# A GRU over 256 steps with an eight-expert layer beside it: first expert products in column groups, one a step

## The chip, the cores and the metric

The kernel runs on one core of a Trainium2 chip. The metric is the device time of one execution in microseconds (us). Three executions of the kernel before took 1025.38, 1026.15 and 1026.09 us, a median of 1026.09 us.

Engines are named as the profile names them: PE is TensorE's matmul side and PEld its weight loads, DVE is VectorE, ACT is ScalarE, POOL is GpSimd, SP is SyncE.

## What is computed

`x` has the shape 16 x 256 x 512 (batch, time, features). A GRU cell runs over the 256 time steps, and its states go through a mixture of eight low-rank experts, of which each token uses the two with the largest router values. The result is added to `x`:

```python
def cell(h, x):
    gi = x @ W_ih + b_ih
    gh = h @ W_hh + b_hh
    r = sigmoid(i_r + h_r)
    z = sigmoid(i_z + h_z)
    n = tanh(i_n + r * h_n)
    return (1.0 - z) * n + z * h
...
router_logits = h / norm(h) @ router_w            # 8 experts, softmax, top 2, renormalised
for e in range(8):
    out = out + combine[:, e, None] * (h @ Wa[e] @ Wb[e])    # 512 -> 128 -> 512
x = x + out
```

Every step needs the state of the step before, so the 256 steps are a chain. The experts do not feed back into it.

## The kernel before, in words

**Numbers in two parts.** Operands of the products are kept as pairs of fp16 numbers, a high and a low part, and each product is three products (`TERMS`: high-high, high-low, low-high). Where two successive products of a pair use the same stationary operand, the second one is a matmul without a weight load (`matmul_held`, line 840); the others go through line 849.

**Steps and blocks.** Eight time steps (S = 8) times 16 batch rows make a block of 128 tokens; there are NB = 32 blocks. In the text "step s" is a time step n with n % 8 = s. PE's program for a step n is: `state_part(n)`, then `wide_step(n)` if n is odd, `grouped_step(n)` if n is even (lines 1081 to 1087).

`state_part(n)` multiplies the state by W_hh. The 16 batch rows of the two parts give 32 stationary columns, so four matmuls, each on 32 columns of the array and 32 partitions of PSUM, run beside each other; I call such four a **quad**. There are 4 quads of 256 moving columns with the first state operand (line 929, which needs `st` from DVE line 762 and the bank seeded by ACT line 570), 4 with the second (line 934), and 8 of 128 columns for the z gate (`zbank`), of which every second is held.

`pair_ahead(n)` computes the input side of the gates for two steps at once, three steps ahead. One pair of steps is 12 **units**, a unit being a quad of 384 columns. `FIRST_UNITS = (3, 5, 5)` says how many units stand in the odd step that begins a pair; the even step after it does the rest. So step 3 has 3 units and step 4 has 9, and all other odd steps have 5 and even steps 7.

The experts' **first products** (`expert_down`, 512 -> 128, one call for one expert and one block) are 12 matmuls of 128 x 128 weights on the whole array, with 128 moving columns, into `ybank`. `DOWN` places them two at a time in steps 1, 3, 5 and 7. The **second products** (`expert_up_by_tokens`, 128 -> 512) are 3 terms of a quad of 512 columns, into `nbank` or `obank`. `UP` places them two at a time in steps 4, 6, 0 and 2. In an odd step the order on PE is state part, router (step 3 alone, `route`), first products, units; in an even step it is state part, units, second products. The last two steps and `last_experts` finish the last block.

**The other engines.** DVE's `gru_step` (lines 732 to 764) transposes the gates' bank (`tr`, line 734), adds the two halves of the r gate (line 737), transposes and adds the rest (740, 742, 745), multiplies by r (749, `rhn`), adds the input's part (753, `npre`), and after ACT's tanh makes the new state (758 `u`, 762 `st`, 763, 719). ACT's `gru_step` makes r (598, `rr`), z (604), 1 - z (606, `omz`), tanh (608, `nn`), and seeds the banks of the next step (570, 577). Each engine then does the `beside(n)` work:
- DVE: turn the input side of the n gate (769), `add_expert(n - 12)` (798, `acc`, one expert a step, on the result of the second product), and in step 3 the two largest router values (776, 778).
- ACT: in even steps the biases (589); in step 7 the squares (617); for every first product `split_y`, two activations (643 and 647); in step 0 two gathers of 512 columns (623); in step 3 `weigh` (638), which waits for POOL's `gaps`; step 2 and 6 convert x.
- POOL: for every first product `low_y` (459), the low part of y; in steps 4 and 6 half of the low part of x (434); in steps 0 to 4 the norm and the router's small work.

Two waits of DVE are touched by the change. Before `npre` (line 753) stand two waits, for `n_turned` (line 751) and for `rhn_ready` (line 752); before `u` (line 758) stands one, for `n_ready`:

```python
dve.wait_ge(n_turned, n // 2 + 1)
dve.wait_ge(rhn_ready, n + 1)
nc.vector.tensor_tensor(npre[:, :, :], rhn[:, :, :], gi_n[...], ALU.add)
...
dve.wait_ge(n_ready, n + 1)
nc.vector.scalar_tensor_tensor(out=u[:, :], in0=nn[:, :], ...)
```

Of the kernel before, what the change touches and what calls it, by code (L numbers as in the profile page):

```python
# [12 lines left out]
P = 128  # L13
# [15 lines left out]
def gru_moe_kernel(nc, x, cond, W_ih, W_hh, b_ih, b_hh, router_w, Wa, Wb, out):  # L29
# [4 lines left out]
    NB = T // S  # L34


    DOWN = (9, 9, 11, 11, 13, 13, 15, 15)
    UP = (12, 12, 14, 14, 16, 16, 18, 18)
    FIRST_UNITS = (3, 5, 5)
    ADD = S + 4  # L40
    YB = 6

    AHEAD = 3
# [9 lines left out]
    with ExitStack() as ctx:  # L53
# [106 lines left out]

        def downs_at(n):

            return [n - DOWN[e] + e for e in range(NE) if DOWN[e] % S == n % S and n >= DOWN[e]]

        def ups_at(n):
# [235 lines left out]
        def _(pool):  # L401
# [100 lines left out]
            def beside(n):  # L502
                i, s = n // S, n % S
                if s == 0 and 1 <= i:
                    fold_squares(i - 1)
                    add_squares(i - 1)
                if s in (1, 2) and 1 <= i:
                    less_upper_half(i - 1, s - 1)
                if s == 3 and 1 <= i:
                    invert_norm(i - 1)  # L510
                if s == 4 and 1 <= i:
                    combine(i - 1)
                if s in (4, 6) and 1 <= i and i + 2 < NB:
                    split_x(i + 2, s // 6, n)
                for m in downs_at(n):
                    low_y(m)
                if s == 3 and 1 <= i:
                    gaps(i - 1)
# [19 lines left out]
        def _(act):  # L538
# [57 lines left out]
            def gru_step(n):  # L596
# [2 lines left out]
                                     scale=1 / PROD_SCALE).then_inc(r_ready, 1)  # L599
                if n % S == 3 and n >= S:  # L600
                    read_router(n // S - 1)
                act.wait_ge(z_summed, n + 1)
                zpre = pre[:, ZG, :, :].rearrange("p k b -> p (k b)")
                nc.scalar.activation(zz[:, :, :].rearrange("p k b -> p (k b)"), zpre, ACT.Sigmoid,  # L604
# [44 lines left out]
            def beside(n):  # L649
                i, s = n // S, n % S  # L650
                if s % 2 == 0 and n + 4 < T:
                    put_biases(n // 2 + 2)
                if s == 7:
                    square(i)
                for m in downs_at(n):
                    split_y(m)
                if s == 0 and 1 <= i:
                    for part in range(2):
                        gather_states(i - 1, part)
                if s == 3 and 1 <= i:  # L660
                    weigh(i - 1)
                if s == SPLIT_AT and i + 3 < NB:
                    split_x(i + 3)
                if s == SCALE_AT and 1 <= i and i + 2 < NB:
                    scale_x(i + 2)
                if n == 0:
                    split_first(2)
                if 0 <= n < len(SPLITS) - N_GRU_SPLITS:
                    split_weights(N_GRU_SPLITS + n)
# [34 lines left out]
        def _(dve):  # L704
# [27 lines left out]
            def gru_step(n):  # L732
# [15 lines left out]
                dve.wait_ge(r_ready, n + 1)  # L748
                nc.vector.tensor_tensor(rhn[:, :, :].rearrange("p k b -> p (k b)"), rr[:, :],
                                        pre[:, HN, :, :].rearrange("p k b -> p (k b)"), ALU.mult).then_inc(rhn_ready, 1)  # L750
                dve.wait_ge(n_turned, n // 2 + 1)
                dve.wait_ge(rhn_ready, n + 1)
                nc.vector.tensor_tensor(npre[:, :, :], rhn[:, :, :], gi_n[:, n // 2 % 2, :, n % 2 * B:(n % 2 + 1) * B],
                                        ALU.add).then_inc(npre_ready, 1)
                dve.wait_ge(z_ready, n + 1)
                nc.vector.tensor_tensor(v[:, :, :], zz[:, :, :], hist[:, past(n - 1), :, (n - 1) % S, :], ALU.mult)
                dve.wait_ge(n_ready, n + 1)
                nc.vector.scalar_tensor_tensor(out=u[:, :], in0=nn[:, :], scalar=PART_SCALE, in1=omz[:, :],  # L758
                                               op0=ALU.mult, op1=ALU.mult).then_inc(u_ready, 1)
# [77 lines left out]
        def _(pe):  # L837
# [108 lines left out]
            def route(f):  # L946
# [5 lines left out]
                if f == NB - 1:  # L952
                    pe.wait_ge(acc_done, LEFT - 1)
                else:
                    pe.wait_ge(yhi_ready, f * NE + 2)
                    pe.wait_ge(y32_ready, f * NE + 2)

                wait(pe, router_read, f)
                pe.wait_ge(sq_step, (f + 1) * SQ_STEPS)
# [12 lines left out]
            def wait_first_product(m):  # L972
                f, e = m // NE, m % NE

                wait(pe, yhi_ready, m - 1)
                wait(pe, y32_ready, m - 1)
                if e == 3 and f < NB - 1:
                    pe.wait_ge(router_read, f + 1)
                if e == 0:
                    pe.wait_ge(both_parts_ready, 2 * ((f + 1) * S + 1))  # L980
                if m in wa_split_at:
                    pe.wait_ge(weights_split, splits_before(wa_split_at[m]))

            def expert_down(m):
# [3 lines left out]
                for k in range(K):  # L988
                    for pw, ph in TERMS:
                        mm = product((pw, ph) == (0, 1), y_at(m)[:, 0:P], wa[:, pw, k, e, :],  # L990
                                     hparts[:, f % HB, k, :, ph * B:(ph + 1) * B], n == 0, n == 3 * K - 1)
                        n += 1
                mm.then_inc(y_done, 1)

# [35 lines left out]

            def pair_ahead(n):

                if n + AHEAD < T:
                    first = FIRST_UNITS[0 if n % S in (3, 4) else 2 if n % S in (7, 0) else 1]
                    pair_part((n + AHEAD) // 2, range(first) if n % 2 else range(first if n else 6, K * len(TERMS)))

            def wide_step(n):
                i, s = n // S, n % S
# [2 lines left out]
                for m in downs_at(n):  # L1041
                    expert_down(m)
                pair_ahead(n)

            def grouped_step(n):
                pair_ahead(n)
                for m in ups_at(n):
                    expert_up_by_tokens(m)
                if n == 0:
# [31 lines left out]
            grouped_step(0)  # L1081
            for n in range(1, T):
                state_part(n)
                if n % 2:
                    wide_step(n)
                else:
                    grouped_step(n)
# [23 lines left out]
```

## Time and profile before

| | |
|---|---|
| median of three runs | 1026.09 us |
| the profiled execution, its own time | 1025.33 us |
| its span, first to last instruction | 1023.5 us |
| mean granted TensorE clock | 0.996 of 2.4 GHz |
| busy: PE, PEld | 987.4 us (96%), 669.4 us (65%) |
| busy: DVE, ACT, POOL | 879.4 us, 692.9 us, 287.9 us |

The time of the profiled execution is the span and 1.8 us around it. A busy PE counts each matmul's whole stay in the pipeline (a quad of 128 columns shows 0.22 us while a new quad starts every 0.056 us), so 96% does not say that PE has no room: the starts of its instructions have to be read. The granted clock is full speed but for the start and the last microseconds.

### The profile page before, as it was taken

What the parts mean: (1) busy time and instruction counts of PE and PEld (TensorE: products, weight loads), DVE (VectorE), ACT (ScalarE), POOL (GpSimd) and SP (SyncE); (2) the same over time, 40 slices, a digit from 0 to 9 for tenths busy, and PEclk for the clock granted to TensorE, in tenths of its full rate; (3) what the DMA queues carried; (4) which work ended last, traced back from release to release, by engine and by line L of the source; (5) the groups of instructions that cost most, each with busy time, mean ns of one, the idle gap of its engine ahead of it and who ended that gap; (6) DMA issues with size and microseconds to landing.
All of it is one profiled execution on the core that took longest, in us unless ns stands there. A gap on an engine that the chain in (4) does not pass through costs nothing.

```text
span 1023.5 us, 60856 instructions
## 1 busy us (share of the span) xinstructions
PE 987.4 (96%) x29067; PEld 669.4 (65%) x20799; DVE 879.4 (86%) x3631; ACT 692.9 (68%) x2696; POOL 287.9 (28%) x729
## 2 busy tenths in 40 slices
PE   4789999999999999999999999999999999999997
PEld 2455666666667666666666666666666666666664
DVE  6889888888888888888888888888888888888886
ACT  6677666676766676666677666667666767766663
POOL 1032233232323322323332332332233322223223
PEclk9999999999999999999999999999999999999999
DMA  8321111111111111111101111101111101110000
GB/s 297 88 80 29 30 32 29 26 31 31 28 32 32 27 27 34 27 30 33 28 25 35 29 31 29 32 25 33 29 29 33 30 24 32 30 30 19 14 9 28
DMA packets 49361, 38.84 MB, mean 38 GB/s; under 512 B 34532, under 2 KB 38972, under 8 KB 49084
## 3 DMA queue, kind: packets, MB, share of 16 engines
q1 hardware_dynamic: 48236, 31.41, 11.3%
q8 instruction: 198, 3.24, 1.3%
q10 hardware_dynamic: 848, 3.54, 1.0%
q14 instruction: 79, 0.65, 0.2%
HBM read 18.94 MB, written 8.39 MB: 27 GB/s over the span
## 4 chain that ended last, share of the span: by engine, by line
PE 89%; DVE 6%; DMA 2%; issue 1%; ACT 1%; SPq 0%; POOL 0%; DVEq 0%; POOLq 0%; ACTq 0%
PE pairs L849 16%; PE ybank L849 12%; PE gates L929 12%; PE gates L934 11%; PE pairs L840 7%; PE ybank L840 6%; PE zbank L849 5%; PE zbank L840 5%; PE obank L849 5%; PE nbank L849 5%; PE obank L840 2%; PE nbank L840 2%; DMA whh<-in_L_cond_W_hh 1%; DVE acc L798 1%; DVE tr L734 1%
## 5 line engine op out<-in xcount | busy, mean ns | idle before, releaser
L849 PE MATMUL pairs<-wx,xs 128*32 128x384 f16 x4096 | 281.9, 328 | 0.2 <-DVE wx L714 0.2
L598 ACT ACTIVATE rr<-pre 128x64 f32<-128x64 f32 x256 | 65.2, 255 | 203.0 <-DVE pre L737 202.9
L849 PE MATMUL ybank<-hparts,wa 128*128 128x128 f16 x2048 | 193.9, 219 | 0.6 <-ACT y L647 0.6
L459 POOL TENSOR_TENSOR y<-y 128x128 f16<-128x128 f32 x256 | 105.6, 433 | 276.2 <-ACT y L647 274.8
L849 PEld LDWEIGHTS ybank<-hparts,wa 128*128 128x128 f16 x2048 | 159.9, 98 | 30.1 <-issue 16.0
L840 PE MATMUL ybank<-hparts,wa 128*128 128x128 f16 x1024 | 178.2, 219 | 0.0
L840 PE MATMUL pairs<-wx,xs 128*32 128x384 f16 x2048 | 175.1, 327 | 0.0
L929 PE MATMUL gates<-whh,st 128*32 128x256 f16 x4080 | 157.8, 273 | 17.3 <-DVE st L762 15.9
L849 PEld LDWEIGHTS pairs<-wx,xs 128*32 128x32 f16 x4096 | 109.6, 97 | 94.2 <-issue 54.7
L929 PEld LDWEIGHTS gates<-whh,st 128*32 128x32 f16 x4080 | 98.3, 96 | 97.2 <-ACT gates L570 86.2
L934 PE MATMUL gates<-whh,hparts 128*32 128x256 f16 x4080 | 158.2, 273 | 0.0
L849 PE MATMUL zbank<-whh,hparts 128*32 128x128 f16 x4080 | 146.4, 219 | 0.0
L840 PE MATMUL zbank<-whh,hparts 128*32 128x128 f16 x4080 | 146.4, 219 | 0.0
L734 DVE STREAM_TRANSPOSE tr<-gates 128x256 f32<-128x256 f32 x256 | 114.5, 447 | 20.5 <-PE gates L934 17.5
L849 PEld LDWEIGHTS zbank<-whh,hparts 128*32 128x32 f16 x4080 | 116.1, 97 | 12.9
L934 PEld LDWEIGHTS gates<-whh,hparts 128*32 128x32 f16 x4080 | 112.9, 97 | 0.6
L570 ACT ACTIVATE gates<-pairs,step_rows 128x256 f32<-128x256 f32 x256 | 110.2, 430 | 0.1
L604 ACT ACTIVATE zz<-pre 128x64 f32<-128x64 f32 x256 | 65.6, 256 | 54.9 <-DVE pre L745 51.3
L849 PE MATMUL obank<-wb,y 128*32 128x512 f16 (+1 forms) x980 | 98.9, 379 | 0.0
L758 DVE SCALAR_TENSOR_TENSOR u<-nn,omz 128x64 f32<-128x64 f32 x256 | 57.5, 225 | 47.0 <-ACT nn L608 47.0
L849 PE MATMUL nbank<-wb,y 128*32 128x512 f16 x976 | 97.4, 379 | 0.0
L577 ACT ACTIVATE zbank<-pairs,step_rows 128x128 f32<-128x128 f32 x256 | 85.0, 332 | 0.0
(134 smaller groups left out, 1825.3 us busy)
## 6 DMA issues: line engine op xcount, KB each, us to landing
out<-outb SPq DMA_DIRECT2D x63, 128.0 KB
xin<-in_x SPq DMA_DIRECT2D x58, 128.0 KB
wih<-in_L_cond_W_ih ACTq DMA_DIRECT2D x4, 768.0 KB, 7.8
whh<-in_L_cond_W_hh SPq DMA_DIRECT2D x4, 768.0 KB, 11.9
wih<-in_L_ffn_Wb SPq DMA_DIRECT2D x8, 256.0 KB, 2.7
xs<-xh SPq DMA_TRANSPOSE x116, 3.1
wih<-in_L_ffn_Wa SPq DMA_DIRECT2D x4, 256.0 KB, 4.4
whh<-in_L_ffn_Wa SPq DMA_DIRECT2D x4, 256.0 KB, 2.8
```

What stands on the lines that cost most here:

```text
L459: nc.gpsimd.tensor_tensor(y[:, m % YB, 1, :], y32[:, m % 2, :], y[:, m % YB, 0, :], ALU.subtract).then_inc(ylo_ready, 1)
L570: nc.scalar.activation(gates[:, 0:2 * P], pairs[n // 2 % 2][:, 0:2 * P], ACT.Copy, scale=step_rows[:, q:q + 1]).then_inc(seeded, 1)
L577: nc.scalar.activation(zbank[:, 0:P], pairs[n // 2 % 2][:, 2 * P:3 * P], ACT.Copy, scale=step_rows[:, q:q + 1]).then_inc(z_seeded, 1)
L598: nc.scalar.activation(rr[:, :], pre[:, RG, :, :].rearrange("p k b -> p (k b)"), ACT.Sigmoid, scale=1 / PROD_SCALE).then_inc(r_ready, 1)
L604: nc.scalar.activation(zz[:, :, :].rearrange("p k b -> p (k b)"), zpre, ACT.Sigmoid, scale=1 / PROD_SCALE).then_inc(z_ready, 1)
L734: nc.vector.transpose(tr[:, 0:2 * K, :].rearrange("p (g k) c -> p g k c", k=K), gates[:, 0:2 * P].rearrange("p (g c k) -> p g k c", g=2, k ...
L758: nc.vector.scalar_tensor_tensor(out=u[:, :], in0=nn[:, :], scalar=PART_SCALE, in1=omz[:, :], op0=ALU.mult, op1=ALU.mult).then_inc(u_ready, 1)
L798: nc.vector.scalar_tensor_tensor(out=(outb if e == NE - 1 else acc)[:, :], in0=o_at(m)[:, :], scalar=comb[:, e:e + 1], in1=(xin[:, f % XIN ...
L840: return nc.tensor.add_instruction(mybir.InstMatmult(name=nc.get_next_instruction_name(), engine=mybir.EngineType.PE, start_tensor_calc=start,
L849: return nc.tensor.matmul(out, lhsT, rhs, start=start, stop=stop, skip_group_check=True)
L929: nc.tensor.matmul(gates[32 * j:32 * j + 32, 0:2 * P], st[:, k, :], whh[:, 1, k, j, 0:2 * P], start=False, stop=False, skip_group_check=True)
L934: mm = nc.tensor.matmul(gates[32 * j:32 * j + 32, 0:2 * P], prior[:, k, :], whh[:, 0, k, j, 0:2 * P], start=False, stop=(k == K - 1), skip ...
```

## The change

The first products of experts 0 and 1 stay on the whole array, both in step 3, after the router. Those of experts 2 to 7 become quads of 32 ranks each (`expert_down_by_ranks`: 12 terms of 4 matmuls, 8 of the 12 with loads), one a step in steps 4, 5, 6, 7, 0 and 1. Second products come one a step (4, 5, 6, 7, 0, 1, and two in step 2). The units of the pairs are dealt out anew: 6 in steps 7, 0, 1 and 2, 3 in step 3, 7 in steps 4, 5 and 6 (a pair begun in step 3 is now ended in step 5). ACT's `weigh` moves into `gru_step` of step 4 behind `rr`; `split_y` goes ahead of `square`; the second gather goes from step 0 to step 1. POOL leaves `low_y` out of step 0 and does it in step 1. DVE's wait for `n_turned` before `npre` stays in step 6 alone and, in steps 1, 3 and 7, stands before the wait for `n_ready` ahead of `u`.

```diff
-    DOWN = (9, 9, 11, 11, 13, 13, 15, 15)
-    UP = (12, 12, 14, 14, 16, 16, 18, 18)
-    FIRST_UNITS = (3, 5, 5)
+    DOWN = (11, 11, 12, 13, 14, 15, 16, 17)
+    UP = (12, 13, 14, 15, 16, 17, 18, 18)
+    UNITS = (12, 6, 12, 3, 10, 5, 12, 6)
...
+            if n >= T - 2:
+                return ((LEFT, LEFT + 1), (LEFT + 2, LEFT + 3))[n - T + 2]
...
-                for m in downs_at(n):
+                for m in (downs_at(n - 1) + downs_at(n) if s == 1 else [] if s == 0 else downs_at(n)):
                     low_y(m)
...
                 if n % S == 3 and n >= S:
                     read_router(n // S - 1)
+                if n % S == 4 and n >= S:
+                    weigh(n // S - 1)
...
+                for m in downs_at(n):
+                    split_y(m)
                 if s == 7:
                     square(i)
-                for m in downs_at(n):
-                    split_y(m)
-                if s == 0 and 1 <= i:
-                    for part in range(2):
-                        gather_states(i - 1, part)
-                if s == 3 and 1 <= i:
-                    weigh(i - 1)
+                if s in (0, 1) and 1 <= i:
+                    gather_states(i - 1, s)
...
-                dve.wait_ge(n_turned, n // 2 + 1)
+                if n == 0 or n % S == 6:
+                    dve.wait_ge(n_turned, n // 2 + 1)
                 dve.wait_ge(rhn_ready, n + 1)
...
+                if n % 2 and n % S != 5 and n + 1 < T:
+                    dve.wait_ge(n_turned, (n + 1) // 2 + 1)
                 dve.wait_ge(n_ready, n + 1)
...
-                    pe.wait_ge(yhi_ready, f * NE + 2)
-                    pe.wait_ge(y32_ready, f * NE + 2)
+                    wait(pe, yhi_ready, f * NE)
+                    wait(pe, y32_ready, f * NE)
...
-                if e == 3 and f < NB - 1:
+                if e == 1 and f < NB - 1:
                     pe.wait_ge(router_read, f + 1)
...
+            def expert_down_by_ranks(m):
+                f, e = m // NE, m % NE
+                wait_first_product(m)
+                n = 0
+                for k in range(K):
+                    for pw, ph in TERMS:
+                        for g in range(4):
+                            of = slice(32 * g, 32 * g + 32)
+                            mm = product((pw, ph) == (0, 1), y_at(m)[of, 0:P], wa[:, pw, k, e, of],
+                                         hparts[:, f % HB, k, :, ph * B:(ph + 1) * B], n == 0, n == 3 * K - 1, 32, 32 * g)
+                        n += 1
+                mm.then_inc(y_done, 1)
...
-                if n + AHEAD < T:
-                    first = FIRST_UNITS[0 if n % S in (3, 4) else 2 if n % S in (7, 0) else 1]
-                    pair_part((n + AHEAD) // 2, range(first) if n % 2 else range(first if n else 6, K * len(TERMS)))
+                s, p, all_units = n % S, (n + AHEAD) // 2, K * len(TERMS)
+                if n % 2 and n > 1 and UNITS[s - 1] < all_units:
+                    pair_part(p - 1, range(UNITS[s - 1], all_units))
+                if p < T // 2:
+                    pair_part(p, range(UNITS[s]) if n % 2 else range(UNITS[s - 1] if n else 6, UNITS[s] if n else all_units))
...
             def wide_step(n):
...
                 pair_ahead(n)
+                for m in ups_at(n):
+                    expert_up_by_tokens(m)
 
             def grouped_step(n):
                 pair_ahead(n)
+                for m in downs_at(n):
+                    expert_down_by_ranks(m)
...
-                if n % 2:
+                if n % S == 3 or n == T - 1:
                     wide_step(n)
```

## Rows read from the trace of the kernel before

**Rows 1.** The page: its span, and the chain that ended last, by engine.

```profile
span 1023.5 us, 60856 instructions
...
PE 89%; DVE 6%; DMA 2%; issue 1%; ACT 1%; SPq 0%; POOL 0%; DVEq 0%; POOLq 0%; ACTq 0%
```

**Rows 2.** PE's timeline (start us, length us): state parts' starts, steps 5, 6, 7, 0, 1, 3, 4, 5.

```profile
505.72 0.61 PE L929 MATMUL gates<-whh,st 128*32 128x256 f16 x16
...
509.43 0.62 PE L929 MATMUL gates<-whh,st 128*32 128x256 f16 x16
...
513.18 0.62 PE L929 MATMUL gates<-whh,st 128*32 128x256 f16 x16
...
516.90 0.62 PE L929 MATMUL gates<-whh,st 128*32 128x256 f16 x16
...
520.87 0.62 PE L929 MATMUL gates<-whh,st 128*32 128x256 f16 x16
...
528.34 0.62 PE L929 MATMUL gates<-whh,st 128*32 128x256 f16 x16
...
532.10 0.61 PE L929 MATMUL gates<-whh,st 128*32 128x256 f16 x16
...
536.17 0.61 PE L929 MATMUL gates<-whh,st 128*32 128x256 f16 x16
```

**Rows 3.** Timelines of DVE and then ACT in step 5, the end of the recurrence.

```profile
507.94 0.22 DVE L749 TENSOR_TENSOR rhn<-rr,pre 128x64 f32<-128x64 f32 x1
508.25 0.23 DVE L753 TENSOR_TENSOR npre<-rhn,gi_n 128x64 f32<-128x64 f32 x1
...
508.80 0.23 DVE L758 SCALAR_TENSOR_TENSOR u<-nn,omz 128x64 f32<-128x64 f32 x1 [0.19 <-ACT nn L608]
509.06 0.23 DVE L762 TENSOR_TENSOR st<-u,v 128x64 f16<-128x64 f32 x1
...
508.21 0.24 ACT L606 ACTIVATE omz<-pre 128x64 f32<-128x64 f32 x1
508.51 0.26 ACT L608 ACTIVATE nn<-npre 128x64 f32<-128x64 f32 x1
```

**Rows 4.** PE's timeline in steps 6 and 7: quads, units, second and first products.

```profile
510.30 0.24 PE L849 MATMUL zbank<-whh,hparts 128*32 128x128 f16 x4
...
510.69 0.24 PE L840 MATMUL zbank<-whh,hparts 128*32 128x128 f16 x4
510.75 0.51 PE L849 MATMUL pairs<-wx,xs 128*32 128x384 f16 x8
...
511.89 0.40 PE L849 MATMUL nbank<-wb,y 128*32 128x512 f16 x4
...
514.45 0.24 PE L840 MATMUL zbank<-whh,hparts 128*32 128x128 f16 x4
514.62 0.23 PE L849 MATMUL ybank<-hparts,wa 128*128 128x128 f16 x1
...
516.07 0.35 PE L849 MATMUL pairs<-wx,xs 128*32 128x384 f16 x4
```

**Rows 5.** PEld's timeline, 521.70 to 521.78: the loads of one quad.

```profile
521.64 0.12 PEld L849 LDWEIGHTS zbank<-whh,hparts 128*32 128x32 f16 x4
```

**Rows 6.** Timelines of DVE and then POOL, from step 6 to step 0.

```profile
513.55 0.71 DVE L798 SCALAR_TENSOR_TENSOR acc<-nbank,comb,acc 128x512 f32<-128x512 f32 x1
514.29 0.45 DVE L734 STREAM_TRANSPOSE tr<-gates 128x256 f32<-128x256 f32 x1
514.77 0.23 DVE L737 TENSOR_TENSOR pre<-tr 128x64 f32<-128x64 f32 x1
...
518.49 0.48 DVE L737 TENSOR_TENSOR pre<-tr 128x64 f32<-128x64 f32 x1
...
513.57 0.67 POOL L434 TENSOR_TENSOR xh<-x,xh 128x256 f16<-128x256 f32 x1 [2.71 <-DVE hparts L719]
518.08 0.81 POOL L459 TENSOR_TENSOR y<-y 128x128 f16<-128x128 f32 x2 [3.84 <-ACT y L647]
```

## The prediction, made before the changed kernel was run

> **What bounds the kernel now.** I read three views: the page, PE's timeline, and the timelines of DVE, ACT and POOL over the same block. The page puts 89% of the chain that ended last on PE [rows 1], which reads as "PE is full". The starts of the state parts say otherwise. A block, from one step 5 to the next, takes 30.45 us (536.17 - 505.72), and its steps are uneven [rows 2]: step 5 3.71, step 6 3.75, step 7 3.72, step 0 3.97, steps 1 and 2 together 7.47, step 3 3.76, step 4 4.07. 3.71 is a floor, and it is not PE's. In step 5 `st` ends at 509.06 + 0.23 = 509.29 and the next state part begins at 509.43, 0.14 later; that 0.14 is what comes between a finished state and its first matmul [rows 2, 3]. In step 0 the same holds, with PE empty ahead of it. So a step lasts as long as the longer of two things: the recurrence (PE's gates, DVE, ACT, DVE: 3.71) or PE's own work. I price both for each step.
>
> PE's work [rows 2, 4]: the state part is 510.75 - 509.43 = 1.32; seven units are 511.89 - 510.75 = 1.14, 0.163 each; two second products are 513.18 - 511.89 = 1.29, 0.645 each; together 3.75, which is step 6's whole length: that step is PE's. A quad of 128 columns takes (510.69 - 510.30) / 7 = 0.056, loads in every second quad included. Step 7 is 1.32, then from 514.62 to 516.07 two first products with the change back to column groups (1.45), the change into the whole array ahead of them (514.62 - 514.45 - 0.056 = 0.11), and 5 units (0.82): 3.70, just under the floor. The whole-array visit thus costs some 0.2 us of PE, but in steps 5, 7 and 1 that lies under the recurrence and taking it away by itself gives nothing. Step 4 has 9 units and is PE's: 3.75 + 2 x 0.163 = 4.08.
>
> Step 0's 3.97 is neither. There DVE's add of the r gate takes 0.48 instead of 0.23 (518.49 against 514.77), and POOL's two `low_y` run from 518.08 to 518.89 [rows 6]. The add ends only after POOL does: the two engines get in each other's way, at 0.26 a block. `low_y` is that late because ACT squares before it splits y in step 7.
>
> **The change, part by part.** (1) PE's work. A first product in column groups is 12 quads of 128 columns. No row shows 8 loading quads in 12, with two loading quads in a row. From below it is 12 x 0.056 = 0.67, the whole-array price; nothing makes it cheaper, since the moving columns are the same. From above it is the pace of the gates' quads, which all load: 8 quads from 509.43 to 510.30, 0.109 each [rows 2, 4], so 8 x 0.109 + 4 x 0.056 = 1.10. I take 0.67, as the nearest row is the z gate's, where a load is followed by its matmuls one quad (0.056) later, and the four loads of a quad lie within 0.12 though one alone is some 0.1 long: they go side by side, not in turn [rows 5]. The gates' 0.109 is what 256 moving columns take anyway. Changing between shapes inside column groups costs nothing visible: 510.69 to 510.75 is the usual 0.06 [rows 4].
>
> The Trainium skill has a rule against this: in TensorEngine Tiling (Array Packing), Restrictions and Gotchas, column groups exclude the fast weight load, and in TensorE: Matmul & The Clock Gate, section LDWEIGHTS, a load takes its columns over 1.2 GHz, 27 ns for 32. Served one after another, four loads would be an estimated 0.107 a quad, as long as my upper bound, and the change would lose.
>
> PE's work is then: steps 0, 1, 7: 1.32 + 6 x 0.163 + 0.67 + 0.645 = 3.61. Step 2: 1.32 + 0.98 + 1.29 = 3.59. Step 3: unchanged (router, two whole-array products, 3 units), 3.76. Steps 4, 5, 6: 1.32 + 1.14 + 0.67 + 0.645 = 3.77.
>
> (2) The recurrence. Between `rhn`'s end (508.16) and `npre` lie 0.09, between `u`'s end (509.03) and `st` only 0.03 [rows 3]. Both depend on the instruction just ahead on DVE; `npre` has a second wait. I read the 0.06 to 0.07 as the price of a second wait, which needs an instruction of its own. `nn` starts 0.03 after `npre` ends, and ACT itself could start it 0.16 after `omz` (508.37), so an earlier `npre` passes through to `nn`, `u` and `st`. The wait goes in every step but 6. In steps 1, 3, 7 it is put before `u`, on the same path, and costs the same 0.07 there. So the floor becomes 3.64 in steps 0, 2, 4, 5 and stays 3.71 in 1, 3, 6, 7. Bounds: 0 (the gap is something else) and 0.07.
>
> (3) The stall of step 0 goes. In step 7 one y is split instead of two, and ahead of the square, so `low_y` (half of 0.81) is over some 0.6 us before the add. Bounds 0 and 0.26; I take 0.26. What is late next: nothing on that path, PE has 3.61 to 3.64.
>
> (4) Where I cost nothing. `low_y` now runs in steps 4 to 7 one at a time. The tightest place is step 6, where it follows POOL's x part: 513.57 + 0.67 + 0.41 = 514.65 against the add at 514.77 [rows 6]; 0.1 is left, and if it were not, 0.26 in step 7. The second product now ends PE's step, so `acc` waits for it: its last matmul begins 0.22 before the next state part and is 0.40 long, so `acc` can begin 0.22 to 0.25 after that start and ends at 0.96, while `tr` comes 1.11 after it (514.29 - 513.18) [rows 2, 4, 6]; in step 6 it already runs closer, 514.26 against 514.29. `weigh` falls into ACT's idle time between `rr` and z in step 4; its `comb` is not due before DVE has the new state, and step 4 has 0.13 of slack to PE. The second gather joins one split in step 1, both ahead of ACT's wait for DVE. The pair ended in step 5 is done 1.65 after that step's start, and ACT seeds from it at about 3. The units' restarts add loads but no quads; behind 384 columns they are hidden. 60 more PE instructions a product, six in a block, come out of a queue that in rows 5 already puts out four loads in a few hundredths; if it cannot keep up, that is part of the upper bound of (1). SP's queue is not touched.
>
> **The sum.** The block after: 3.64 (0) + 3.71 (1) + 3.64 (2) + 3.76 (3) + 3 x 3.77 (4, 5, 6) + 3.71 (7) = 29.77, against 30.45: 0.68 less. Of that, evening out steps 4 and 5 gives 0.24, the stall and the wait in step 0 0.33, step 2 0.11. There are 28 full blocks in the steady state; the first three, with weights still converted, and the last one I count as two more. 30 x 0.68 = 20.4. The profiled execution would come to 1025.33 - 20.4 = 1004.9; the median of the runs lies 0.8 above it, so 1005.7.
>
> **The rivals.** (A) Grouped loads at the gates' pace, the slower side. Its place is the load of two quads in a row on PE, its price 0.43 a product. Steps 4 to 6 become 4.20, steps 0, 1, 7 4.04, the block 3 x 4.20 + 3 x 4.04 + 3.64 + 3.76 = 32.12, 1.67 more: 1026.1 + 50 = 1076. It decides from 0.15 a product upwards, because six products, less the slack of 0.03 and twice 0.10, then eat the 0.68. For it: no row has this mix. Against it: rows 4 and 5. 0.09; the skill's rule above is this rival. (B) The second wait is free, or comes back elsewhere: steps 0 and 2 stay at 3.71, 0.14 a block, 1009.9. The rows show the gap, not its cause. 0.13. (C) POOL and DVE still meet: in step 0 or, through step 6's x part, in step 7. One such meeting is 0.26 a block, 1013.5; two make 1021. For it: six places where `low_y` now lies instead of four, with 0.1 at one. 0.14. (D) The change does not do what it says because the steps are the recurrence's, not PE's; then only steps 4 and 5 gain, 0.24, and 1019. This needs the stall and the wait both to stay: 0.04.
>
> **How the numbers follow.** My forecast has 0.60, with 1002 to 1009 for it: the lower end if step 3 gains too or the first blocks gain more, the upper if each grouped product costs some 0.03 more. The range takes in B and one meeting of C: 1001.5 to 1015; left out are A, D and C's second meeting. A measurement of this kernel can tell about 0.2% (2 us) from no change. Faster by more: forecast, B, C and D, 0.90, less a little for partial prices of A that cancel: 0.88. Within: 0.03. Slower: 0.09.
>
> **What would show it.** Starts of the state parts: 3.64 in steps 0 and 2, 3.71 in 1 and 7, 3.77 in 4, 5, 6. Grouped `ybank` quads 0.056 apart, 0.67 a product; 0.109 would mean A. `npre` 0.03 behind `rhn`, and in steps 1, 3, 7 `u` 0.1 behind `nn`; else B. The add at line 737's place at 0.23 in every step; 0.48 anywhere means C. I am wrong if step 4 is still the longest, or if a step without PE's load is over 3.72.

## The result, and the profile after

The changed kernel takes 1033.7 us (median of four runs, 1032.44 to 1036.87); the kernel before took 1025.74 beside it. The ratio is 1.0083, with a 95% interval of [1.0068, 1.0097]: slower by 0.8%, where the prediction was 1005.7. (Times are medians; the ratios are the ones on record with the runs, and the quotient of two medians can differ from them by a few units of the last digits.) In the profiled executions the span grew by 11.6 us, from 1023.5 to 1035.1.

The page of the changed kernel: span, busy times, the instruction queue (packets, MB, share of the DMA engines), the chain by engine, and one row of the costliest groups.

```profile
span 1035.1 us, 71895 instructions
...
PE 982.5 (95%) x35691; PEld 712.0 (69%) x25343; DVE 882.6 (85%) x3631; ACT 695.1 (67%) x2696; POOL 288.1 (28%) x729
...
q8 instruction: 242, 3.96, 1.6%
...
PE 88%; DVE 6%; issue 3%; DMA 2%; ACT 1%; SPq 0%; POOL 0%; DVEq 0%; POOLq 0%
...
L853 PE MATMUL ybank<-hparts,wa 128*32 128x128 f16 (+1 forms) x6464 | 221.1, 219 | 9.2 <-issue 9.2
```

The same row of the page of the kernel before:

```profile
q8 instruction: 198, 3.24, 1.3%
```

Two things moved against [rows 1]: "issue", time in which PE waited for nothing that the profile shows, went from 1% to 3% of the chain, and the queue that brings instructions carried 242 packets instead of 198. 3.96 MB in 242 packets is 16 KB each. The trace holds 61,997 records of PE (matmuls, loads and waits), 256 times 242 and 45 more, so a packet is 256 instructions of 64 bytes; before it holds 50,830, 256 times 198 and 142 more.

First, what went as forecast. PE's timeline of the changed kernel, starts of the state parts in steps 0 to 7 and the next 0, in a block that nothing disturbs:

```profile
681.88 0.62 PE L933 MATMUL gates<-whh,st 128*32 128x256 f16 x16
...
685.53 0.62 PE L933 MATMUL gates<-whh,st 128*32 128x256 f16 x16
...
689.26 0.62 PE L933 MATMUL gates<-whh,st 128*32 128x256 f16 x16
...
692.90 0.62 PE L933 MATMUL gates<-whh,st 128*32 128x256 f16 x16
...
696.66 0.61 PE L933 MATMUL gates<-whh,st 128*32 128x256 f16 x16
...
700.43 0.61 PE L933 MATMUL gates<-whh,st 128*32 128x256 f16 x16
...
704.21 0.61 PE L933 MATMUL gates<-whh,st 128*32 128x256 f16 x16
...
707.98 0.61 PE L933 MATMUL gates<-whh,st 128*32 128x256 f16 x16
...
711.70 0.62 PE L933 MATMUL gates<-whh,st 128*32 128x256 f16 x16
```

The steps are 3.65, 3.73, 3.64, 3.76, 3.77, 3.78, 3.77 and 3.72, the block 29.82; the prediction's were 3.64, 3.71, 3.64, 3.76, 3.77 three times and 3.71, together 29.77. If every block were like this one the kernel would gain some 20 us. The mean block (27 blocks, from the fourth on) is 30.98, though, against 30.49 before. The 29 blocks behind the first two are 13.8 us longer in all, the first two are 2.0 shorter, and the two together are the span's 11.6 to within 0.2.

The lost time sits in the middle of running work. PE's timeline around step 4 to 6 of another block (in brackets: idle before, and what ended it):

```profile
354.98 0.28 PE L853 MATMUL ybank<-hparts,wa 128*32 128x128 f16 x8
355.09 0.23 PE L844 MATMUL ybank<-hparts,wa 128*32 128x128 f16 x4
355.15 0.22 PE L853 MATMUL ybank<-hparts,wa 128*32 128x128 f16 x2
356.02 0.29 PE L853 MATMUL ybank<-hparts,wa 128*32 128x128 f16 x6 [0.65 <-issue]
...
356.86 0.65 PE L933 MATMUL gates<-whh,st 128*32 128x256 f16 x16
...
360.12 0.22 PE L844 MATMUL ybank<-hparts,wa 128*32 128x128 f16 x3 [0.20 <-issue]
...
361.01 0.64 PE L933 MATMUL gates<-whh,st 128*32 128x256 f16 x16
...
364.53 0.24 PE L853 MATMUL ybank<-hparts,wa 128*32 128x128 f16 x3 [0.51 <-issue]
```

A quad is cut in two: two of its matmuls start at 355.15, the other two 0.87 later, though all four depend on the same things. The loads stop with it, as PEld's timeline of the changed kernel shows:

```profile
356.03 0.22 PEld L853 LDWEIGHTS ybank<-hparts,wa 128*32 128x32 f16 x9 [0.83 <-issue]
```

So it is neither an array that is full nor a load that is slow: both sides of TensorE stand still, and the profile shows nothing that they wait for. PE's waits in the changed kernel, by group (us in total, times, longest):

```profile
PE ybank L853 <- issue: 9.2, 22, 0.7
...
PE ybank L844 <- issue: 3.6, 8, 0.7
```

Numbering PE's recorded instructions from 0 (matmuls, loads and waits, in order of start) gives the place. I count a pause from one start to the next, between 130 and 1000 us, leaving out the gates' products, which may be waiting for the state. By this count the changed kernel has 50 pauses of more than 0.23 us inside running work, up to 0.96 us; with the gates' products it has 62, the number in e1's expectation below. All 50 lie right behind an instruction numbered 256k + 192, for one k or another; the kernel before has none, there or elsewhere. They account for the whole loss: what PE's starts lose at these places is 1.12 us a block (every gap over 0.1 there, less the usual 0.056), and the mean block less the quiet one is 30.98 - 29.82 = 1.16. My theory F (fetch) was that PE's instructions come in pieces of 256, one packet of the instruction queue each, that a piece cannot follow the last one sooner than some time, and that PE runs dry when it uses up a piece faster than that. The instructions by step (0 to 7) are 255, 256, 195, 207, 263, 264, 263, 253 in the changed kernel, 1956 a block; before they were 203, 188, 206, 204, 215, 185, 206, 185, 1592 a block. A grouped product issues 80 (48 matmuls, 32 loads), a whole-array one 20.

The rival D (density) was that the fetch halts PE's sequencer for a fixed time at every border, that the instructions queued ahead of PE normally hide it, and that a stretch of short quads, which drains them fast, does not. F follows the count of instructions, wherever they stand; D follows where the short quads are.

### The profile page after: what moved, and what is told of

It reads as the page before. It is cut to its first block, busy times and chain, and to the rows that moved or that the text cites. A ratio compares the mean times of both kernels' runs of the same rounds, so it can differ in the third digit from the quotient of the medians.

```text
span 1035.1 us, 71895 instructions
## 1 busy us (share of the span) xinstructions
PE 982.5 (95%) x35691; PEld 712.0 (69%) x25343; DVE 882.6 (85%) x3631; ACT 695.1 (67%) x2696; POOL 288.1 (28%) x729
## 3 DMA queue, kind: packets, MB, share of 16 engines
q8 instruction: 242, 3.96, 1.6%
## 4 chain that ended last, share of the span: by engine, by line
PE 88%; DVE 6%; issue 3%; DMA 2%; ACT 1%; SPq 0%; POOL 0%; DVEq 0%; POOLq 0%
PE pairs L853 16%; PE ybank L853 12%; PE gates L933 11%; PE gates L938 10%; PE pairs L844 7%; PE ybank L844 6%; PE zbank L844 5%; PE nbank L853 5%; PE zbank L853 5%; PE obank L853 5%; PE obank L844 2%; PE nbank L844 2%; DVE acc L802 1%; DMA whh<-in_L_cond_W_hh 1%; DVE tr L735 1%
## 5 line engine op out<-in xcount | busy, mean ns | idle before, releaser
L853 PE MATMUL pairs<-wx,xs 128*32 128x384 f16 x4224 | 295.8, 326 | 0.3 <-DVE wx L715 0.2
L853 PE MATMUL ybank<-hparts,wa 128*32 128x128 f16 (+1 forms) x6464 | 221.1, 219 | 9.2 <-issue 9.2
L853 PEld LDWEIGHTS ybank<-hparts,wa 128*32 128x32 f16 (+1 forms) x6464 | 185.1, 97 | 54.3 <-issue 26.5
L844 PE MATMUL ybank<-hparts,wa 128*32 128x128 f16 (+1 forms) x3232 | 193.5, 219 | 3.6 <-issue 3.6
L853 PEld LDWEIGHTS pairs<-wx,xs 128*32 128x32 f16 x4224 | 129.2, 97 | 83.1 <-issue 47.4
L933 PE MATMUL gates<-whh,st 128*32 128x256 f16 x4080 | 162.5, 273 | 18.4 <-DVE st L766 17.4
L844 PE MATMUL pairs<-wx,xs 128*32 128x384 f16 x1920 | 172.8, 326 | 0.0
L933 PEld LDWEIGHTS gates<-whh,st 128*32 128x32 f16 x4080 | 105.6, 96 | 85.8 <-ACT gates L572 61.5
L938 PE MATMUL gates<-whh,hparts 128*32 128x256 f16 x4080 | 163.2, 273 | 0.1
L853 PE MATMUL zbank<-whh,hparts 128*32 128x128 f16 x4080 | 152.3, 219 | 1.0 <-issue 0.9
L844 PE MATMUL zbank<-whh,hparts 128*32 128x128 f16 x4080 | 152.1, 219 | 0.4 <-issue 0.2
L853 PEld LDWEIGHTS zbank<-whh,hparts 128*32 128x32 f16 x4080 | 121.4, 97 | 14.5 <-issue 3.2
L853 PE MATMUL nbank<-wb,y 128*32 128x512 f16 x976 | 102.2, 379 | 0.8 <-issue 0.6
```

Of the source, the lines that this page charges most:

```text
L844: return nc.tensor.add_instruction(mybir.InstMatmult(name=nc.get_next_instruction_name(), engine=mybir.EngineType.PE, start_tensor_calc=start,
L853: return nc.tensor.matmul(out, lhsT, rhs, start=start, stop=stop, skip_group_check=True)
L933: nc.tensor.matmul(gates[32 * j:32 * j + 32, 0:2 * P], st[:, k, :], whh[:, 1, k, j, 0:2 * P], start=False, stop=False, skip_group_check=True)
L938: mm = nc.tensor.matmul(gates[32 * j:32 * j + 32, 0:2 * P], prior[:, k, :], whh[:, 0, k, j, 0:2 * P], start=False, stop=(k == K - 1), skip ...
```

## The experiments

**e1: the change without column groups.** The whole new plan stays, but the six products run on the whole array.

```diff
             def grouped_step(n):
...
                 for m in downs_at(n):
-                    expert_down_by_ranks(m)
+                    expert_down(m)
```

> The changed kernel with all first products on the whole array again, its schedule kept. The trace of the changed kernel shows PE standing still only between its recorded instructions 256k+192 and the next, for up to 0.9 us (62 times over 0.23 us), and its steps otherwise at the predicted lengths. Theory F (fetch): PE's program arrives in pieces of 256 instructions (the packets of 16 KB in the instruction queue, 242 against 198 before), one at a time, and a piece cannot follow the last one sooner than some 3.6 to 4.3 us; 1956 instructions a block instead of 1592 come too close to that. Here a block has about 1596, so F expects no such pause, and steps 0, 1, 7 at 3.82, steps 4 to 6 at 3.98 (0.21 of change of array mode each), 2 at 3.64, 3 at 3.76: a block of 30.8 us and 1033 to 1037 us in all. Theory D (density): each border of a piece costs a fixed halt, hidden by the 64 or so instructions already queued unless they are the quick quads of a first product; D too expects no pauses here. If the pauses stay, both are wrong and the schedule or the semaphores cause them.

Measured: 1038.25 us, 1.0127 [1.0110, 1.0144], 1.25 above the range given. 1596 instructions a block and no pause that goes by 256k + 192. (Its only gaps over 0.23 us inside running work are 168 of 0.25 us, each between a unit and the first matmul of a whole-array product, wherever the number of the instruction falls: there the array changes its shape.) Its page, the instruction queue and the chain:

```profile
q8 instruction: 199, 3.26, 1.3%
...
PE 91%; DVE 5%; DMA 2%; ACT 1%; issue 1%; SPq 0%; POOL 0%; DVEq 0%; POOLq 0%
```

and its PE timeline, three state parts:

```profile
506.56 0.61 PE L933 MATMUL gates<-whh,st 128*32 128x256 f16 x16
...
510.56 0.61 PE L933 MATMUL gates<-whh,st 128*32 128x256 f16 x16
...
514.60 0.62 PE L933 MATMUL gates<-whh,st 128*32 128x256 f16 x16
```

"Issue" is back at 1%, the packets at 199, and the steps with a lone product are long: 4.00 and 4.04 here, in steps 4 and 5, and 3.83 in steps 7, 0 and 1. Each lone product now pays for two changes of the array's shape. The pauses came with the column groups, and without them the plan is worse still. 4.00 is 0.23 over the 3.77 of the changed kernel, near the 0.2 that the prediction put on a visit. Both theories expected no pauses here, so this run does not tell them apart. In step 5 `tr` starts 1.50 after the state part instead of 1.10, which I did not follow up.

**e2: more instructions where no quad is short.** The held quads of the units (384 columns) and of the second products (512 columns) get weight loads that they don't need; the first products are as they were.

```diff
             def pair_part(...):
-                        mm = product((ph, pw) == (0, 1) and unit > units[0], bank[...],
+                        mm = product(False, bank[...],
...
             def expert_up_by_tokens(m):
-                        mm = product((ph, pw) == (0, 1), o_at(m)[rows, :], ...
+                        mm = product(False, o_at(m)[rows, :], ...
```

> The changed kernel with every held quad of the units and of the second products given its own weight loads: about 92 PE instructions more a block (1956 to 2048, eight pieces), all of them under 384 or 512 moving columns, so the array's own work is the same. F: eight pieces a block at 3.9 to 4.2 us each, 31.2 to 33.6 us a block against 31.0: slower by 7 to 80 us, 1040 to 1110 us, with more pauses at the borders. D: the added loads stand in slow stretches, nothing changes, 1030 to 1038 us.

Measured: 1052.98 us over two runs, 1.0269 [1.0248, 1.0289], 83 pauses, all at 256k + 192. Its page:

```profile
q8 instruction: 253, 4.15, 1.6%
...
PE 88%; DVE 5%; issue 3%; ACT 2%; DMA 1%; ACTq 0%; DVEq 0%
```

19 us more than the changed kernel, from loads that lie under 384 and 512 moving columns and add no work to the array. D gave 1038 at most, and it falls; the measured time is in the lower part of what F gave. The loads are free by themselves: steps 4 and 5 take 3.775 (median) where no border disturbs them, as in the changed kernel. No block is undisturbed any more, so even the shortest, 30.56, holds four gaps; the mean block, 31.44, less the 1.65 that PE loses at the borders is 29.79.

**e3: column groups in the kernel before.** All eight first products by ranks, everything else as before.

```diff
             def wide_step(n):
...
-                    expert_down(m)
+                    expert_down_by_ranks(m)
```

> The kernel before with its eight first products a block in column groups and nothing else changed: 480 PE instructions more a block, 1592 to 2072. F: 8.1 pieces a block at 3.9 to 4.2 us, 31.6 to 34 us a block against 30.5: 1060 to 1130 us. D: a halt where a border falls into the 160 quick instructions of an odd step, about 2.5 borders a block, 0.3 to 0.8 each less the slack: 1040 to 1060 us. If neither holds, the odd steps stay at the recurrence's 3.71 and the time at 1026.

Measured: 1089.28 us over two runs, 1.0623 [1.0602, 1.0644], inside F's range and far over D's; 73 pauses, all at 256k + 192, 61.7 us together. Its page, the queue, the chain, and the group of the first products:

```profile
q8 instruction: 256, 4.19, 1.6%
...
PE 88%; issue 6%; DVE 3%; DMA 2%; ACT 0%; SPq 0%; POOL 0%; DVEq 0%; POOLq 0%
...
L849 PE MATMUL ybank<-hparts,wa 128*32 128x128 f16 (+1 forms) x8000 | 208.3, 219 | 35.8 <-issue 34.9
```

Two grouped products in one step hold 160 instructions in some 1.3 us (24 quads of 0.056). The shortest block, 30.52, is within 0.07 of the one of before: nearly all that the groups cost is the pauses.

**e4: the same count, spread out.** In the changed kernel each grouped product's 12 quads are dealt three at a time between the units of its step.

```diff
+                    if unit % 3 != 1 and between:
+                        between.pop(0)()
...
-                pair_ahead(n)
                 for m in downs_at(n):
-                    expert_down_by_ranks(m)
+                    between.extend(expert_down_by_ranks(m))
+                pair_ahead(n)
```

> The changed kernel with the 12 quads of each grouped product dealt out, three at a time, between the units of its step: the same instructions, but nowhere more than 20 quick ones in a row. F: the number of instructions a block is the same, so the time is the changed kernel's, 1030 to 1038 us, though the pauses may stand elsewhere. D: the queued 64 instructions now last about 1 us everywhere, the pauses go, 1004 to 1012 us.

Measured: 1031.67 us over ten runs, 1.0056 [1.0034, 1.0079], 41 pauses, all at 256k + 192. They go wherever the border falls, into the z gate for instance, as e4's PE timeline shows:

```profile
336.61 0.23 PE L853 MATMUL zbank<-whh,hparts 128*32 128x128 f16 x2 [0.25 <-issue]
```

D wanted the pauses gone and 1004 to 1012. The time is 2 us under the changed kernel's, which is within the spread (this kernel's runs go from 1026.2 to 1037.8, and the two intervals overlap), and F's range holds it: the loss stays with the count.

**e5: the two waits of DVE alone**, in the kernel before.

```diff
+                if n == 0 or n % S == 6:
                 dve.wait_ge(n_turned, n // 2 + 1)
...
+                if n % 2 and n % S != 5 and n + 1 < T:
+                    dve.wait_ge(n_turned, (n + 1) // 2 + 1)
                 dve.wait_ge(n_ready, n + 1)
```

> The kernel before with the two edits of DVE's waits alone. If a second wait ahead of an instruction costs 0.07 us on the recurrence, npre follows rhn after 0.03 instead of 0.10 in all steps but 6, u follows nn 0.07 later in steps 1, 3 and 7, steps 0 and 5 get shorter by 0.07 and 0.02 and the others, bound by PE or with the wait put back, do not: 1022 to 1023.5 us. If the gap is something else: no change.

Measured: 1023.1 us over ten runs, 0.9978 [0.9968, 0.9988]. DVE's timeline of e5, step with the second wait gone:

```profile
502.61 0.22 DVE L749 TENSOR_TENSOR rhn<-rr,pre 128x64 f32<-128x64 f32 x1
502.87 0.22 DVE L754 TENSOR_TENSOR npre<-rhn,gi_n 128x64 f32<-128x64 f32 x1
```

`npre` starts 0.26 after `rhn`, against 0.31 in [rows 3], and 0.04 after its end; over all blocks the gap is 0.03 where the second wait is gone and 0.10 where it stays (medians). Where the wait was put before `u`, the way from the start of `nn` to the state's end is 0.85 instead of 0.77. So a second wait costs 0.07 to 0.08, in either place.

**e6: the split of y ahead of the squares, alone**, in the kernel before.

```diff
-                if s == 7:
-                    square(i)
                 for m in downs_at(n):
                     split_y(m)
+                if s == 7:
+                    square(i)
```

> The kernel before with ACT splitting y ahead of the square in step 7, nothing else. If the stall of step 0 is POOL's low_y running into DVE's add of the r gate, the add is back at 0.23 us and step 0 falls from 3.98 to PE's 3.75: 1018 to 1020 us. If ACT's own lateness is the cause, the square now delays r instead and nothing is gained.

Measured: 1018.22 us, 0.9929 [0.9915, 0.9943]. POOL's and then DVE's timeline of e6 in step 0:

```profile
514.50 0.82 POOL L459 TENSOR_TENSOR y<-y 128x128 f16<-128x128 f32 x2 [3.27 <-ACT y L647]
...
515.48 0.22 DVE L737 TENSOR_TENSOR pre<-tr 128x64 f32<-128x64 f32 x1
```

POOL is done 0.16 before DVE's add begins; the add takes 0.22 instead of the 0.48 of [rows 6], and step 0 3.75 instead of 3.98. Two swapped calls gave 7.0 us (1025.24 beside it), near the 30 x 0.26 = 7.8 that the forecast counted for the stall, and need no column groups.

**e9: 32 instructions a block fewer.** The changed kernel, with the z gate's products taken in the order k = 3, 0, 1, 2: its first quad then finds its weights still loaded by the gates' last quad and needs no loads.

```diff
-                for k in range(K):
+                for k in (K - 1, 0, 1, 2):
...
-                            mm = product(pw == 1, zbank[...],
+                            mm = product(pw == 1 or k == K - 1, zbank[...],
```

> The changed kernel with four weight loads a step fewer (the z gate starts on the weights that the r gate loaded last): 1924 PE instructions a block instead of 1956, nothing else. F: 0 to 8 us under the changed kernel's 1033.7, 1026 to 1033 us, as e8 was 2 us under e7. D: 1033 us.

Measured: 1023.1 us over ten runs, 0.9975 [0.9962, 0.9987], with 32 pauses of 17.6 us together. The columns moved are the same and so is the shortest block (29.81), yet it is 10.6 us faster than the changed kernel. That is below the range I gave, because I had priced it by the pauses it might avoid; D gave no gain at all. By the count it is 32 / 256 of a piece a block at some 4.05 us (below), 0.51, and over 31 blocks 15.7; measured 10.6.

**e7: two array visits**, and **e8: the same with e9's order.** In e7 experts 2 and 3 are taken two in step 7's whole-array visit, four stay in groups.

```diff
-    DOWN = (11, 11, 12, 13, 14, 15, 16, 17)
-    UP = (12, 13, 14, 15, 16, 17, 18, 18)
-    UNITS = (12, 6, 12, 3, 10, 5, 12, 6)
+    DOWN = (11, 11, 12, 13, 15, 15, 16, 17)
+    UP = (12, 13, 14, 14, 16, 17, 18, 18)
+    UNITS = (12, 6, 12, 3, 10, 5, 12, 5)
...
-                if n % S == 3 or n == T - 1:
+                if n % S in (3, 7):
```

> A version that should beat both if theory F holds: the changed kernel, but experts 4 and 5 on the whole array together in step 7, so that four instead of six products are in column groups: 1836 PE instructions a block instead of 1956. By PE and the recurrence: steps 0 3.78, 1 3.71, 2 3.64, 3 3.76, 4 and 5 3.775, 6 3.75, 7 3.71, a block of 29.9 us and 1006 us in all. F: a piece of 256 instructions lasts 4.2 us on the mean, but 3.7 where steps 4 and 5 lie in one, so some pauses stay: 1006 to 1014 us. D: pauses per grouped product as before, four sixths of them: 1015 to 1025 us.

> The kernel of e7 with the z gate starting on the state quarter whose weights the last quad of the r gate has just loaded, so that four weight loads a step go: 1804 PE instructions a block, the array's work unchanged. F: fewer pauses than e7, 1 to 4 us faster than it, 1005 to 1011 us. D: no difference to e7.

Measured: e7 1017.57 us, 0.9938 [0.9917, 0.9959], 11 pauses; e8 1015.31, 0.9895 [0.9880, 0.9911], 7 pauses. Both gain, and both stand above what F gave: I had counted on fewer pauses than there are, and with 7.17 and 7.05 pieces a block some stretches still run dry. e7's time lies in the range that D gave, so e7 by itself does not speak against D; e2, e3, e4 and e9 do. The step between the two, 2.3 us for 32 instructions, is a fifth of e9's, since most borders here have room.

**e10: three array visits.** Four products stay in groups no longer: two visits more (steps 5 and 7), two products in groups (steps 0 and 1), e9's order, units finished ahead of a whole-array visit, DVE's `turn_n` in other steps, and DVE's wait for `n_turned` moved ahead of the add that stands at line 742 of the kernel before, in even steps alone.

```diff
+    DOWN = (11, 11, 13, 13, 15, 15, 16, 17)
+    UP = (12, 12, 14, 14, 16, 17, 18, 18)
+    UNITS = (10, 5, 12, 3, 10, 3, 10, 3)
...
+                if n % 2 == 0:
+                    dve.wait_ge(n_turned, n // 2 + 1)
...
-                if s in (0, 2, 5, 6) and n // 2 + 1 < T // 2:
-                    turn_n(n // 2 + 1, n + 2 if s == 5 else 0)
+                if s in (1, 2, 5, 7) and n // 2 + 1 < T // 2:
+                    turn_n(n // 2 + 1, n + 2 if s != 2 else 0)
...
+                if n % S in (3, 5, 7):
```

> A version built on both findings: whole-array visits of two products in steps 3, 5 and 7, column groups only for experts 6 and 7 in steps 0 and 1; units dealt out as 3, 7, 5, 7, 5, 7, 7, 7 over steps 3 to 2, the end of a pair ahead of the whole-array products; DVE's wait for n_turned on the add at line 743, where nothing waits for it; the held quad of e8. About 1690 PE instructions a block. By PE and the recurrence: steps 0 3.77, 1 3.77, 2 3.75, 3 3.76, 4 3.75, 5 3.69, 6 3.75, 7 3.69, a block of 29.93 us. F: a piece lasts 4.5 us on the mean and two quick ones never follow each other, so hardly a pause: 1008 to 1012 us, and the runs lie close together. If pauses stay as in e8: 1012 to 1016 us.

Measured: 1009.87 us (1009.45 to 1010.79), 0.9856 [0.9840, 0.9873], the fastest of all. Its page:

```profile
span 1008.1 us, 63738 instructions
...
q8 instruction: 210, 3.44, 1.5%
...
PE 89%; DVE 6%; ACT 2%; DMA 1%; issue 1%; ACTq 0%; DVEq 0%; POOL 0%; POOLq 0%
```

and its PE timeline, from step 1 to the next step 1, first and last start and two between:

```profile
481.30 0.61 PE L931 MATMUL gates<-whh,st 128*32 128x256 f16 x16
...
492.57 0.61 PE L931 MATMUL gates<-whh,st 128*32 128x256 f16 x16
...
503.77 0.61 PE L931 MATMUL gates<-whh,st 128*32 128x256 f16 x16
...
511.24 0.61 PE L931 MATMUL gates<-whh,st 128*32 128x256 f16 x16
```

This block is 29.94, the mean 30.06: slower at its best than the changed kernel's 29.82, and 0.92 better on average, because only two pauses are left. Several things changed at once here, so this is a version built on the findings and no test of one of them.

**e11: what needs no column groups at all.** The kernel before with e6's edit and the wait for `n_turned` moved as in e10.

```diff
+                if n % 2 == 0:
+                    dve.wait_ge(n_turned, n // 2 + 1)
...
-                dve.wait_ge(n_turned, n // 2 + 1)
                 dve.wait_ge(rhn_ready, n + 1)
```

> The kernel before with the two parts of the change that paid alone, ACT's order in step 7 and no second wait before npre (the wait for n_turned now on line 742's add in even steps, none before u): 1592 PE instructions a block, no column groups. Steps 0 3.75, 1 3.70, 2 3.75, 3 3.76, 4 4.08, 5 3.69, 6 3.75, 7 3.70, a block of 30.18 us: 1015 to 1017 us.

Measured: 1013.66 us, 0.9893 [0.9876, 0.9909]. Of e10's 15 us, 11 can be had this way, without column groups. The steady block is the 30.18 expected; the time is below the range given, and the first three blocks, 1.7 us shorter together, are where more was gained than I had counted.

**All of it by the count.** Instructions on PE a block, pieces of 256, the shortest and the mean block (from state part to state part, 27 blocks from the fourth on), the mean block divided by its pieces, and the pauses counted as above, those at 256k + 192:

| kernel | instr. | pieces | shortest | mean | us a piece | pauses |
|---|---|---|---|---|---|---|
| before | 1592 | 6.22 | 30.45 | 30.49 | 4.90 | 0 |
| e1 | 1596 | 6.23 | 30.91 | 31.01 | 4.97 | 0 |
| e10 | 1692 | 6.61 | 29.94 | 30.06 | 4.55 | 2 |
| e8 | 1804 | 7.05 | 29.92 | 30.28 | 4.30 | 7 |
| e7 | 1836 | 7.17 | 29.93 | 30.30 | 4.22 | 11 |
| e9 | 1924 | 7.52 | 29.81 | 30.57 | 4.07 | 32 |
| e4 | 1956 | 7.64 | 29.82 | 30.84 | 4.04 | 41 |
| after | 1956 | 7.64 | 29.82 | 30.98 | 4.05 | 50 |
| e2 | 2048 | 8.00 | 30.56 | 31.44 | 3.93 | 83 |
| e3 | 2072 | 8.09 | 30.52 | 32.55 | 4.02 | 73 |

From 7.5 pieces a block on, a piece takes 3.93 to 4.07 us whatever the plan is. The changed kernel's own work would need one every 29.82 / 7.64 = 3.90, and in steps 4 to 6 one every 3.67: it asks for more than comes.

## Why the prediction was wrong

**Part (4), the instructions costed at nothing: the step that failed.** It set the 60 more PE instructions a product, six in a block, at nothing because four loads leave a queue in a few hundredths, and let the upper bound of (1) stand for the case that the queue can't keep up. That row shows how fast instructions leave a queue that is full, not how fast it is filled. Filling goes by pieces of 256, and its price is not paid per product but per piece, wherever the border falls. It came to 30.98 - 29.82 = 1.16 a block, 0.19 a product: inside the bound of 0.43, and over the 0.15 from which the prediction itself had the change lose. With the 1.16 against the 0.68 forecast as gain, the block is some 0.5 longer, as measured. The warning was in the trace of before: 198 packets, and no piece of 256 that PE used up in less than 4.28 us. Steps 4 to 6 of the changed kernel would have a border every 256 / 263 x 3.775 = 3.67, closer than anything the trace had shown to be possible.

**Parts (1) to (3) and the sum: right.** Grouped quads start 0.056 apart. Where no border disturbs them steps 4 to 6 take 3.775 at the median (3.77 forecast), steps 0 and 2 3.65 (3.64), steps 1 and 7 3.73 and 3.72 (3.71), and the sum of the undisturbed block missed by 0.05. Part (2): DVE's timeline of the changed kernel in step 5:

```profile
702.70 0.22 DVE L750 TENSOR_TENSOR rhn<-rr,pre 128x64 f32<-128x64 f32 x1
702.95 0.23 DVE L755 TENSOR_TENSOR npre<-rhn,gi_n 128x64 f32<-128x64 f32 x1
```

0.03 behind, as forecast, `u` 0.11 behind `nn` in steps 1, 3 and 7 (0.1 forecast), and e5 shows by itself that it is the wait. Part (3): the add takes 0.22 in step 0 and nowhere more than 0.29, and e6 shows by itself that the order of split and squares did it; alone it gave 7.0 us.

**The rivals.** A had the right sign, slower, for the wrong reason. Loads are not slow: eight of twelve quads load, and the quads are still 0.056 apart, not 0.109. The Trainium skill's rule behind it (TensorEngine Tiling (Array Packing), Restrictions and Gotchas: no fast weight load with column groups) does not show as four loads in a row here; the trace disagrees with the estimate of 0.107 a quad that the prediction worked out beside it. B fell with e5, C and the prediction's D (not the density of above) with the quiet block, where every step is as forecast. None of the rivals had the instructions' supply as a mechanism of its own, so the chance of 0.88 for faster was that of a sum that left a resource out. (The four chances that it adds up to 0.90 come to 0.91; nothing hangs on it.)

## What to carry to other kernels

Count the instructions of an engine over a stretch, not only their durations: in these runs PE was given 256 of them in some 4.0 us, about 63 a us, and a plan that asks for more pauses at borders 256 apart, as idle time put down to "issue" in the middle of a quad. Compare the shortest time in which the trace shows 256 of them used up with what the change would need, before trusting a sum of durations. Column groups cost four times the instructions of the whole array for the same columns (80 against 20 a product here), so use them where a step has few others (e10), and test the small edits beside a big one by themselves: here they held most of the gain.

## What the runs showed of the hardware that I had not expected

How a piece arrives, from the instruction queue's records and PE's numbered instructions. For the borders of the kernel after between 330 and 377 us (times in us; landing is the end of the piece's packet, counted from the moment PE reached the border):

```
border    landing   pause
330.270   -1.641    none
333.966   -1.377    none
337.725   -0.959    0.477
341.775   -1.054    0.313
345.730   -1.210    0.385
351.040   -2.613    none
355.153   -0.624    0.872
359.705   -1.018    0.415
363.801   -0.624    0.726
368.103   -0.901    0.457
372.135   -0.470    0.851
376.560   -0.687    0.726
```

In these rows the packet has always landed before PE gets there, and PE still pauses: landing and pause together come to 1.32 to 1.60 us, so a piece can be used only about 1.40 us (median at the pauses) after its packet is in. The three rows without a pause have 1.377, 1.641 and 2.613 in hand; in the kernel before, the least in hand is 1.93. So the pause is no fixed halt, as D had it: it is as long as the packet is late. At the pauses the next packet begins 1.36 us (median) after PE has entered a piece, and the packets ahead of a pause take 1.26 (all packets between 130 and 1000 us: 1.10), which makes 1.36 + 1.26 + 1.40 = 4.02 in all; the distance of two borders that both paused is 4.10 at the median. That the three parts follow each other is read from these records; no run changed one of them. What asks for a packet isn't shown: in the changed kernel every one between 130 and 1000 us begins after PE has entered the piece, 0.04 to 3.06 us after, but in the kernel before 24 of 178 begin before PE gets there, by up to 0.9 us. Whether less other DMA traffic would shorten the packets wasn't tried, and why some of them start late stays open.

The Trainium skill says in Runtime: NRT & Kernel Launch, Instruction fetch mechanics, that the sequencer fetches blocks of 256 instructions over a DMA queue of its own while it works on the current one, which the 242 packets bear out, and that crossing a border is mostly hidden since instructions are issued more slowly than they come in. In the kernel before that holds; in the changed one, e2 and e3 it does not, and there the measurement decides.
